# A GNN message pass: counting messages at a fixed address, with one offset load per packed round

## The reference

```python
all_msgs = jnp.einsum('nh,thd->ntd', h, message_W) + message_b
msg = all_msgs[src, edge_type]
messages = jax.ops.segment_sum(msg, dst, num_segments=num_nodes)
gi = messages @ gru_w_ih.T + gru_b_ih
gh = h @ gru_w_hh.T + gru_b_hh
i_r, i_z, i_n = jnp.split(gi, 3, axis=-1)
h_r, h_z, h_n = jnp.split(gh, 3, axis=-1)
r = jax.nn.sigmoid(i_r + h_r)
z = jax.nn.sigmoid(i_z + h_z)
n = jnp.tanh(i_n + r * h_n)
return (1.0 - z) * n + z * h
...
x = _layernorm(x + _L0_gnn_ref(...), axis=-1)
```

## Time and profile before

| what | us |
|---|---|
| median of 3 runs | 2053.66 |
| lowest and highest of them | 2050.83, 2055.22 |
| span of the profiled execution | 2554.5 |
| POOL busy in it | 1495.5 (59%) |
| PE busy in it | 1716.8 (67%) |
| DVE and ACT busy in it | 1114.2 (44%), 583.5 (23%) |

### The profile page before, as it was taken

The page is one execution under the profiler, slowest core; times in us unless marked ns, Lnnn a source line. Parts: engine busy times, 40 slices in busy tenths (PEclk is TensorE's granted clock), DMA queues, the critical chain, the costliest instruction groups (busy, mean ns, idle before and its releaser), DMA issues.

```text
span 2554.5 us, 36262 instructions
## 1 busy us (share of the span) xinstructions
PE 1716.8 (67%) x8072; PEld 1287.4 (50%) x8073; DVE 1114.2 (44%) x3736; ACT 583.5 (23%) x1662; POOL 1495.5 (59%) x1592
## 2 busy tenths in 40 slices
PE   1554646766777776775767777776777776677777
PEld 1544534545555554554555555554555555555555
DVE  6576254343444444443344343434343434343444
ACT  2212412222221212121212121222122221212121
POOL 5566565555666665665666665655565655656663
PEclk9776667767776777677777677777777776767667
DMA  3111111111111111111111111111111111111111
GB/s 97 43 51 51 42 48 49 47 49 47 52 47 51 48 51 46 51 49 43 50 51 48 51 49 50 51 48 47 50 50 48 52 46 51 48 49 48 51 48 33
DMA packets 96778, 126.99 MB, mean 50 GB/s; under 512 B 31138, under 2 KB 71009, under 8 KB 96752
## 3 DMA queue, kind: packets, MB, share of 16 engines
q0 software_dynamic: 50560, 103.65, 14.4%
q1 hardware_dynamic: 45994, 23.03, 3.3%
q10 hardware_dynamic: 198, 0.00, 0.0%
HBM read 120.15 MB, written 6.40 MB: 50 GB/s over the span
## 4 chain that ended last, share of the span: by engine, by line
PE 31%; issue 28%; another core or an unknown queue 19%; DVE 10%; ACT 8%; DVEq 3%; ACTq 1%; DMA 0%; SPq 0%
PE msg L1564 10%; PE agg L1538 7%; PE cnt L1517 4%; PE gates L1613 3%; ACT sums_room L672 3%; PE turn L1592 2%; DVEq L1073 2%; ACT agg L672 1%; PE gates L1607 1%; DVE onehot L1066 1%; ACT loops L672 1%; PE gates L1606 1%; DVE work L1093 1%; DVE messages_T L1082 1%
## 5 line engine op out<-in xcount | busy, mean ns | idle before, releaser
L608 POOL DMA_INDIRECT rows<-in_x_dram,idx x1392 | 1314.6, 944 | 902.2 <-ACT idx L672 518.2
L1564 PE MATMUL msg<-sums_room,w_type 128*128 128x320 f32 (+1 forms) x1552 | 599.1, 557 | 222.1 <-issue 217.9
L1538 PE MATMUL agg<-onehot,rows 128*128 128x128 f32 x3124 | 558.2, 341 | 69.2 <-issue 64.6
L1564 PEld LDWEIGHTS msg<-sums_room,w_type 128*128 128x128 f32 x1552 | 388.3, 259 | 417.1 <-issue 365.6
L1538 PEld LDWEIGHTS agg<-onehot,rows 128*128 128x128 f32 x3124 | 500.7, 243 | 104.9 <-issue 95.7
L1082 DVE TENSOR_TENSOR messages_T<-messages_T,msg 128x64 f32 x291 | 64.6, 222 | 464.6 <-issue 227.0
L1066 DVE TENSOR_TENSOR onehot<-code_T,codes 128x640 f32<-128x640 f32 (+1 forms) x294 | 244.8, 862 | 29.3 <-PE agg L1538 12.1
L1592 PE MATMUL turn<-loops,spread 16*128 16x128 bf16 x696 | 78.7, 241 | 241.1 <-ACT loops L672 187.8
L1111 DVE TENSOR_TENSOR sums_room<-turn,x_turned 128x512 f32<-128x512 f32 x173 | 119.6, 691 | 277.8 <-PE turn L1592 135.8
L672 ACT ACTIVATE idx<-src_T 128x5 int32 (+3 forms) x261 | 52.4, 201 | 810.0 <-remote 728.6
L608 POOL DMA_INDIRECT rows<-in_x_dram,src_T x170 | 161.9, 952 | 117.2 <-PE agg L1538 68.4
(11 more groups left out here) (208 smaller groups left out, 1316.6 us busy)
## 6 DMA issues: line engine op xcount, KB each, us to landing
rows<-in_x_dram,idx POOLq DMA_INDIRECT x1392
x_next<-in_x_dram SPq DMA_DIRECT2D x97, 64.0 KB
out_dram<-out_tile SPq DMA_DIRECT2D x97, 64.0 KB
x_tile<-in_x_dram SPq DMA_DIRECT2D x96, 64.0 KB
rows<-in_x_dram,src_T POOLq DMA_INDIRECT x170
work<-in_dst_dram SPq DMA_DIRECT2D x1, 609.4 KB
work<-in_src_dram SPq DMA_DIRECT2D x1, 609.4 KB
work<-in_edge_type_dram SPq DMA_DIRECT2D x1, 609.4 KB
```

What stands on the lines that cost most here:

```text
L608: nc.gpsimd.indirect_dma_start(out=to, out_offset=None, in_=x[:, :], in_offset=bass.IndirectOffsetOnAxis(ap=index, axis=0),).then_inc(done ...
L1538: last = nc.tensor.matmul(agg[c][:, ds(offs[c][k] * TYPES, CODES)], (rows_second if second else rows)[:, start + k, :], onehot[c][:, k, :] ...
L1564: nc.tensor.matmul(msg[:, 0:cols], w_type[:, t, :], sums[:, t, 0:cols], start=t == 0, stop=False, skip_group_check=True)
```

## The change

Packed rounds (11 to 97) are changed in four ways. `offsets(r)` issues one load of the round's 16 offsets in place of three loads; the offset of each group's first tile is taken as the constant 0. `count_tiles` writes 64 columns at a fixed address for every tile, and the first matmul of a group overwrites (`start=k == 0`); so the masks of DVE are 64 wide and no register is used. ACT no longer clears the count columns, and copies the turned node tile ahead of the counts. For that, `rel_T` must hold a node's place in the group's window and not in the tile's span: in round 10 DVE copies the offsets to three fp32 rows, PE spreads each row over the 128 partitions with a matmul against ones (`spread_offsets`), and DVE adds it to `rel_T`. `code_T`, which the sums use, is computed before that and keeps the old numbering; the sums still write at register addresses. Early rounds keep their form.

```diff
+        offset_lots = [(row, a, min(row.shape[1], SPARE_TILE + 1 - a))
+                       for row, a in ((gate_bias, 0), (bias_rest, 512), (bi_row, 1024))]
...
-                copy(counts[:, :, :], cnt[:, 0:3 * WINDOW].rearrange("p (c n) -> p c n", c=3)).then_inc(counts_read, 1)
-                if since(r, 1):
+                if since(r, EARLY):
                     copy_turned(r - 1)
-                act.wait_ge(counts_read, r + 1)
-                zero_counts().then_inc(counts_copied, 1)
+                read = copy(counts[:, :, :], cnt[:, 0:3 * WINDOW].rearrange("p (c n) -> p c n", c=3))
+                if since(r, EARLY):
+                    read.then_inc(counts_copied, 1)
+                else:
+                    read.then_inc(counts_read, 1)
+                    if since(r, 1):
+                        copy_turned(r - 1)
+                    act.wait_ge(counts_read, r + 1)
+                    zero_counts().then_inc(counts_copied, 1)
...
-                    cols = ds(column(r, start), n)
+                    cols, wide = ds(column(r, start), n), SPAN if early(r) else WINDOW
                     nc.vector.tensor_tensor(
-                        node_mask[c][:, 0:n, :], rel_T[:, cols].unsqueeze(2).broadcast_to([P, n, SPAN]),
-                        codes[:, 0:SPAN].unsqueeze(1).broadcast_to([P, n, SPAN]), ALU.is_equal)
+                        node_mask[c][:, 0:n, 0:wide], rel_T[:, cols].unsqueeze(2).broadcast_to([P, n, wide]),
+                        codes[:, 0:wide].unsqueeze(1).broadcast_to([P, n, wide]), ALU.is_equal)
...
+                dve.wait_ge(packed_offset_ready, 4)
+                for row, a, n in offset_lots:
+                    nc.vector.tensor_copy(row[0:1, 0:n], offset_packed[0:1, a:a + n]).then_inc(packed_offset_ready, 1)
                 dve.wait_ge(packed_code_ready, 1)
+                for lot, (_, a, n) in enumerate(offset_lots):
+                    cols = slice(EARLY_TILES + a, EARLY_TILES + a + n)
+                    dve.wait_ge(offset_spread, lot + 1)
+                    nc.vector.tensor_tensor(rel_T[:, cols], rel_T[:, cols], turn[:, 0:n], ALU.add).then_inc(offset_added, 1)
+                dve.wait_ge(offset_added, len(offset_lots))
...
                 for c, n, start in groups(r):
-                    values = offset_early if early(r) else offset_packed
-                    a = column(r, start) if early(r) else packed(r, start)
-                    _, group = nc.values_load_multi_w_load_instructions(
-                        values[0:1, ds(a, n)], engines=[pe.engine], min_val=0, max_val=WINDOW - SPAN,
-                        skip_runtime_bounds_check_because="checked on the chip before this path is taken")
-                    offs.append(group)
+                    offs.append((0, *every[start + 1:start + n]))
...
+                        else:
+                            last = nc.tensor.matmul(cnt[:, c * WINDOW:(c + 1) * WINDOW], type_mask[c][:, k, :],
+                                                    node_mask[c][:, k, :], start=k == 0, stop=True, skip_group_check=True)
...
+            def spread_offsets():
+
+                for lot, (row, _, n) in enumerate(offset_lots):
+                    pe.wait_ge(packed_offset_ready, 5 + lot)
+                    wait_used(pe, offset_added, lot)
+                    nc.tensor.matmul(turn[:, 0:n], ones[0:1, :], row[0:1, 0:n], start=True, stop=True).then_inc(offset_spread, 1)
...
+                if isinstance(r, int) and r == EARLY - 1:
+                    spread_offsets()
                 if since(r, LAG):
                     make_gates(r - LAG)
```

More of the change, by code:

```diff
@@ L189, in gnn_kernel @@
         b_wide = rows_second[:, 0:TYPES, :].rearrange("p t d -> p (t d)")
-        node_mask = [sb(f"node_mask{c}", [P, n, SPAN], BF16) for c, n in enumerate(EARLY_GROUPS)]
+        node_mask = [sb(f"node_mask{c}", [P, n, WINDOW], BF16) for c, n in enumerate(EARLY_GROUPS)]
         type_mask = [sb(f"type_mask{c}", [P, n, P], BF16) for c, n in enumerate(EARLY_GROUPS)]
@@ L302, in gnn_kernel @@
         packed_offset_ready = sem("packed_offset_ready")
-        loops_zero = sem("loops_zero")
-        spread_ready = sem("spread_ready")
+        offset_spread = sem("offset_spread")
+        offset_added = sem("offset_added")
         gathered = [sem(f"gathered{k}") for k in range(EARLY_ROUND)]
@@ L1025, in _ @@
                 spread[:, :, :], iota_f[0:2 * TYPES, TYPES:2 * TYPES].unsqueeze(2).broadcast_to([2 * TYPES, TYPES, P]),
-                own_row[0:2 * TYPES, 0:1], None, ALU.is_equal).then_inc(spread_ready, 1)
+                own_row[0:2 * TYPES, 0:1], None, ALU.is_equal).then_inc(codes_ready, 1)
             dve.wait_ge(bad_summed, 1)
@@ L1281, in mark_last_tile @@
                 nc.vector.tensor_tensor(
-                    node_mask[1][:, k:k + 1, :], rel_T[:, cols].unsqueeze(2).broadcast_to([P, 1, SPAN]),
-                    codes[:, 0:SPAN].unsqueeze(1).broadcast_to([P, 1, SPAN]), ALU.is_equal).then_inc(last_tile_ready, 1)
+                    node_mask[1][:, k:k + 1, :], rel_T[:, cols].unsqueeze(2).broadcast_to([P, 1, WINDOW]),
+                    codes[:, 0:WINDOW].unsqueeze(1).broadcast_to([P, 1, WINDOW]), ALU.is_equal).then_inc(last_tile_ready, 1)
                 nc.vector.tensor_tensor(
@@ L1322, in round_ @@
                     dve.wait_ge(fields_turned, FIELDS * CHUNKS)
-                    nc.vector.tensor_scalar(
+                    step(nc.vector.tensor_scalar(
                         loops_T[:, :].rearrange("p (n w) -> p n w", w=P),
                         codes[0:2 * TYPES, 0:P].unsqueeze(1).broadcast_to([2 * TYPES, ACC_ROWS // P, P]), 0.0, None,
-                        ALU.mult).then_inc(loops_zero, 1)
-                    dve.wait_ge(loops_zero, 1)
+                        ALU.mult))
                 if since(r, EARLY - 1):
@@ L1494, in offsets @@
                 offs = []
-                for c, n, start in groups(r):
-                    values = offset_early if early(r) else offset_packed
-                    a = column(r, start) if early(r) else packed(r, start)
-                    _, group = nc.values_load_multi_w_load_instructions(
-                        values[0:1, ds(a, n)], engines=[pe.engine], min_val=0, max_val=WINDOW - SPAN,
-                        skip_runtime_bounds_check_because="checked on the chip before this path is taken")
-                    offs.append(group)
+                if early(r):
+                    for c, n, start in groups(r):
+                        _, group = nc.values_load_multi_w_load_instructions(
+                            offset_early[0:1, ds(column(r, start), n)], engines=[pe.engine], min_val=0, max_val=WINDOW - SPAN,
+                            skip_runtime_bounds_check_because="checked on the chip before this path is taken")
+                        offs.append(group)
+                    return offs
+                _, every = nc.values_load_multi_w_load_instructions(
+                    offset_packed[0:1, ds(packed(r, 0), ROUND)], engines=[pe.engine], min_val=0, max_val=WINDOW - SPAN,
+                    skip_runtime_bounds_check_because="checked on the chip before this path is taken")
+                for c, n, start in groups(r):
+                    offs.append((0, *every[start + 1:start + n]))
                 if isinstance(r, int) and r == LAST:
@@ L1516, in count_tiles @@
                     for k in range(n):
-                        last = nc.tensor.matmul(cnt[:, ds(offs[c][k] + c * WINDOW, SPAN)], type_mask[c][:, k, :],
-                                                node_mask[c][:, k, :], start=False, stop=True, skip_group_check=True)
+                        if early(r):
+                            last = nc.tensor.matmul(cnt[:, ds(offs[c][k] + c * WINDOW, SPAN)], type_mask[c][:, k, :],
+                                                    node_mask[c][:, k, 0:SPAN], start=False, stop=True, skip_group_check=True)
+                        else:
+                            last = nc.tensor.matmul(cnt[:, c * WINDOW:(c + 1) * WINDOW], type_mask[c][:, k, :],
+                                                    node_mask[c][:, k, :], start=k == 0, stop=True, skip_group_check=True)
                 if isinstance(r, int) and r == LAST:
                     pe.wait_ge(last_tile_ready, 2)
-                    last = nc.tensor.matmul(cnt[:, ds(offs[3][0] + 2 * WINDOW, SPAN)], type_mask[1][:, GROUPS[1], :],
+                    last = nc.tensor.matmul(cnt[:, 2 * WINDOW:3 * WINDOW], type_mask[1][:, GROUPS[1], :],
                                             node_mask[1][:, GROUPS[1], :], start=False, stop=True, skip_group_check=True)
@@ L1586, in spread_loops @@
                 elif isinstance(r, int) and r == EARLY:
-                    pe.wait_ge(spread_ready, 1)
+                    pe.wait_ge(codes_ready, 2)
+                    pe.wait_ge(offset_added, len(offset_lots))
                     pe.wait_ge(fields_copied, FIELDS * CHUNKS)
```

1 line of the change is left out of this document (added).

## The result

The changed kernel takes 2022.2 us (median of 4 runs, 2020.8 to 2024.4) against 2054.4 for the kernel before: a ratio of 0.985, interval 0.983 to 0.986, or 32 us less. The forecast was 2056, the range began at 2030. The time fell by more than the 10 us that the prediction named as its refutation.

What follows compares the result with a forecast made beforehand. The prediction took POOL's gathers to bound the timed kernel, PE's chain just underneath: 2053.66 + 0 (loop) + 5.0 (numbering) - 1 (end) = 2057.7, or 2053.7 with 4 recovered in the loop; set at 2056, range 2030 to 2065.

Steps and rivals of the forecast that it cites:

- the term for the loop: Packed rounds: PE's shorter chain stays hidden under POOL's 19.95 us in each of 86 rounds; 0, bounds 0 and -4.
- the undisturbed round: Traced round at 521: 22.13 us less 1.74 of ACT waiting for ended sums, so PE's chain is some 20.4 us.
- Rival B: Packed rounds: PE's chain still decides in part, so the loop gives back time, 2049 or about 2015; chance 0.32.
- B's larger form: Packed rounds: an untraced gather takes 1.22 us, the loop gives back 43 us, about 2015; chance 0.11 down to 2010.
- The loads: PE ahead of the turn of x: one load takes 1.3 us, the 2.3 us gap falls by about 2 a round.
- The counts: PE's sixteen count matmuls in a packed round: 1.5 us in place of 2.07, a gain of 0.5.
- The masks: DVE's three mask operations, four times as wide: from 0.25 to some 0.5 us each, +0.8 us a round.
- rival D: Loop: wider masks hinder the gathers; at 0.03 us per gather 42 us more, 2095; chance 0.04.
- PE's chain: Packed rounds: loads, counts, ACT and DVE together make it some 2.8 us shorter, 17.2 in place of 20.0.
- The numbering: Round 10, between the last offset and PE's weights: +5.5 us, bounds +4 and +7.5; +5.0 after shorter counts.
- the end: Last round, 17 counts without registers when no gathers are left: -1 us, bounds -2 and 0.
- rival C: Round 10: DVE's path sets the restart after the numbering, +8 to +12 us, 2062 to 2066; chance 0.14.

Runs made afterwards that it cites:

- e15: The kernel before with fifteen gathers in a packed round in place of sixteen, against the kernel before: 2053.4 us against 2055.0, ratio 1.000.
- e17: The changed kernel with fifteen gathers in a packed round in place of sixteen, against the changed kernel: 1918.9 us against 2022.2.
- e9: The changed kernel, unchanged, measured again against the kernel before: 2021.7 us against 2054.6, ratio 0.984.
- e18: The changed kernel with the turn of x done nine times in a packed round, against the changed kernel: 2021.7 us against 2021.7 and 2022.2.

## Why the prediction was wrong

**The step that failed** is the sum by which I took the timed kernel to be bound by gathers: 4.61 + 1969.0 + 18.7 + 32.5 + 11.8 + 8.7 = 2045.3, leaving 8.4. I had just called PE's pauses something that the timed executions don't have, and then carried over into the sum the holes and the tail of the very execution that had them, with "causes outside PE's pauses". They had none that the timed executions share. e15, the nearest to the timed kernel, has 3.6 (the hole at 50.16 less its fixed 0.30) in place of 18.7 and nothing in place of 11.8. Behind the last gather it has 2049.5 - 2021.73 - 1.25 = 26.5 and the load alone 24.3, in place of 32.5. That takes 15.1 + 11.8 + 6.0 to 8.2 = 33 to 35 us out of the sum. The 8.4 us left for launch and waits in the loop become 41 to 44, some 0.5 in each of 86 rounds. That is the 20.47 against 19.95, and most of the 39.6 that the load alone gained. So the term for the loop, put at 0 with -4 as its bound, was about -41. The agreement to within 8 us was chance.

**The number that was right and was overruled** is the undisturbed round, 22.13 - 1.74 = 20.4. e15 measures 20.47, and the 1.74 us of ACT's idleness show on PE as a longer wait for the loops, 3.16 us in that round of the kernel before for 1.51 in e15:

```profile
537.51 0.39 PE L1592 MATMUL turn<-loops,spread 16*128 16x128 bf16 x4 [3.16 <-ACT loops L672]
```

But the chain isn't PE's alone, as the prediction had it: it leads through DVE and ACT. Rival B gave just this case, at 0.5 us a round and "about 2015", but tied it to shorter gathers; the gathers stayed 1.25 apart and it was the holes that shrank. B's larger form got 0.11.

**The loads**: I took 1.3 us for the one load; it is 1.106, as the view of the tile of offsets in the changed kernel has it (ns, shortest, median and longest):

```profile
L1519 PEldq TENSOR_LOAD <-offset_packed x87: 1102/1106/1120, 265.9 to 1983.7; - x87
...
L1525 PEldq TENSOR_LOAD <-offset_packed x1: 313/313/313, 1984.9 to 1984.9; - x1
```

The gap ahead of the turn of x was 3.03 us on the timed kind of chip (257.9 / 85), not 2.3, and is gone. The direction and the mechanism stand; only the worth, 0, fell with the bound. By the Trainium skill (Runtime: NRT & Kernel Launch, Instruction fetch mechanics), about 200 ns for each register, the one load would take 3.2 us (an estimate), and against the 3.3 us of the three the load alone would have gained next to nothing. It took 1.106, 69 ns for each of sixteen values, and gained 39.6 us. The measurement decides against a fixed price for each register.

**The counts**: 1.06 us, inside the 1 to 1.7 named. That the load alone frees the register steps too I hadn't seen. **The masks**: 0.55 and 0.48 us, as said, and gathers beside them keep 0.94, so rival D is out. **PE's chain** "some 2.8 us shorter": e17 has it at 18.72 or below, from 20.47, so by 1.7 at least; how much exactly wasn't measured.

**The numbering** was about right, **the end** was not. The rows of the changed kernel in round 10:

```profile
259.21 0.14 DVE L1282 TENSOR_TENSOR offset_packed<-work 1x1 int32<-1x1 int32 x1
...
259.85 2.07 PE L1664 MATMUL turn<-gate_bias,ones 1*128 1x512 f32 x2 [14.52 <-DVE gate_bias L1287]
...
262.86 2.04 PE L1664 MATMUL turn<-bias_rest,ones 1*128 1x512 f32 x2 [0.94 <-DVE rel_T L1292]
...
265.78 1.57 PE L1664 MATMUL turn<-bi_row,ones 1*128 1x369 f32 x2 [0.87 <-DVE rel_T L1292]
...
270.24 4.17 PE L1590 MATMUL msg<-sums_room,w_type 128*128 128x192 f32 x16
```

From the last offset to the weights it is 270.24 - 259.35 = 10.9 us; I said 9.1. The three matmuls took 2.07, 2.04 and 1.57, my upper bounds, not 1.8, 1.8 and 1.3, and the gates before the weights 2.9 for 2.2. POOL restarts 19.5 us behind the last offset, 18.9 in e9 (17 to 19 said), and 13.5 in e15, which has the three loads: 5.4 to 6.1 later, for +5.5 forecast, and rival C's price of 8 to 12 wasn't reached. Against the load alone, which restarts 10.8 behind the last offset since its weights don't wait for three loads, the price is higher: POOL restarts 278.89 - 269.42 = 9.5 us later. At the end the changed kernel gets 24.3 - 20.6 = 3.7 back, where the sum had -1 and -2 as its bound (other profiles with fixed counts end in 20.4 to 22.7, so part of the 3.7 varies). The two leave 5.8 of the 6.6 us that lie between the medians of the load alone and the changed kernel.

**What would show it**: the profiled span fell by 535 us, not by 150 to 300, but that compares the two kinds of execution and shows nothing.

**Still open**: why some chips run this kernel with pauses of PE's sequencer and 25% longer, and why the load alone gains 39 us on one of them and loses 23 on another.

## What to carry to other kernels

A profile and a time can come from two occasions on which the kernel behaves differently. Where a profiled span is far from the timed one, a sum that mixes rows of the first with the median of the second proves nothing, and a term that is "explained" must not be taken from the disturbed stretch.

Where two chains are within 3% of each other (20.47 and 19.95 here), ask each by taking work out of it: one gather less gained 1.6 us before the change and 103 after it. And of a change with two parts that both shorten the same chain, try each alone: here the load by itself reached the next bound, and the second part only added a net 6.6 us outside the loop.

## What the hardware showed

One load of sixteen registers takes 1.11 us on PE and one of a single register 0.31, where loads of six, five and five values took 0.82, 1.24 and 1.23: sixteen that begin at a multiple of sixteen cost less than five that begin at place 6 or 11.

PE's granted clock was the lower behind a row of waits for gathers. The same gates, 384 columns twice, took 0.91 us in e15 and 1.65 in the changed kernel; these are the stretches (us, busy us of PE and PEld, DVE, ACT, POOL, then PE's clock, DMA share, GB/s) from the changed kernel, then from e15:

```profile
1000.30:1004.90 4.60, 4.60 (x17) 2.88 (x17) 2.15 (x4) 1.29 (x3) 3.38 (x5) 0.50 0.18 46
```

```profile
1007.80:1013.30 5.50, 2.38 (x14) 1.52 (x15) 3.89 (x8) 2.05 (x7) 3.98 (x6) 1.00 0.19 48
```

In the first PE had just gone five times through a wait of 0.4 to 0.9 us for a gather and ran at 1.2 GHz, in the second it had worked through its sums without waiting for one and ran at 2.4; behind its 3.01 us of waiting for loads it fell as well, to 0.66 over the counts. And with the eight transposes of e18 the counts took 0.63 us and the sums of the first group 1.58, without them 1.06 and 2.13: the clock was back at 1.00 when the counts began, 0.50 without them, and 1.60 us more of work made the work behind it about 1 us shorter.

A gather took 2.54 us in place of 0.94 in the changed kernel beside the operation that makes `code_T`, which reads two SBUF tensors (2.13 before the change); beside the wider masks of the loop gathers took 0.95 us on average.
